# Attention and expert layer on one core: TensorE weighs the older group directly behind the new group's scores and turns the slot's probabilities afterwards

## The chip, the cores and the metric

The kernel runs on one core of one Trainium2 chip. Its time is the device time of one execution in microseconds (us). It is float32 throughout. TensorE is called PE, VectorE DVE, ScalarE ACT, GpSimd POOL and SyncE SP.

## The reference

One decoder layer over x of 16 sequences x 256 positions x 512 features: a self-attention with three softmaxes, a cross-attention with a relative band, and a layer of product-key experts. The change touches the cross-attention alone. Cut to that:

```python
q = (wq @ query + bq); k = (wk @ key + bk); v = (wv @ value + bv)   # 8 heads of 32 channels, 512 positions
scores = einsum('bhqd,bhkd->bhqk', q, k) * scale
scores = scores + skew(einsum('bhqd,rd->bhqr', q, rel_k)) * ...      # a band of 9 offsets
weights = softmax(where(mask == 0, -inf, scores))
context = einsum('bhqk,bhkd->bhqd', weights, v) + band(weights) @ rel_v
out = wo @ context + bo
```

## The kernel before

Everything up to about 1413 us is the attention pass; the expert pass follows it. The attention pass is a software pipeline of rounds over the 16 sequences (b runs from -1 to 17). A round has 32 steps s. In each step every engine takes its part from a list written out by hand (`round_` of each engine, with the table `At` of steps at which the other work stands). Each engine works strictly in its written order; semaphores join them.

A round of the cross-attention makes 32 softmax tiles of 128 queries x 512 keys (8 heads x 4 query tiles), in 8 groups of 4 heads. The path of a tile is:

- **score** (PE, L705): at every fourth step, the four heads of a group at once, each in a 32-row part of the array, into four PSUM banks (h_bank and s_bank in the trace). It waits until DVE has taken the last scores of the group before out of the banks (semaphore `s_emptied`).
- **top_score** (DVE, L1243): adds mask and band and takes the maximum (nmx), one head per step. It waits for the score, and for the exponential of two steps before, whose buffer it writes.
- **exponentials** (ACT, L1054): one per step.
- **turn** (PE, L715): three steps later, four transposes of 128x128 into one of two PSUM banks `t_bank`. The two banks are given out in turn to turns and other products (REL, CK, CQ, CV, PB), so a job waits until the job two before it has been copied out.
- **turned** (ACT, L1060): copies that bank to SBUF. In ACT's list of a step it is the first thing; the exponential stands behind it, and the copies that the self-attention wants (L975, L1022, L1002, L982 and others) stand behind the exponential.
- **weigh** (PE, L731): eight steps behind the score, 16 products in 32-column parts of the array (32 instructions in the trace, two for each) that weigh the values of a whole older group; it needs the turned probabilities up to step s-2 and `linv_kept` (L1065, a copy made two steps before). DVE takes its result one step later (L1261, `evict`).

Between these stand the products of the self-attention of another sequence, which go through one PSUM bank `a_bank`: XN (two sets of transposes, L743, steps 0 and 1), Q (steps 2 to 5), RAW, V, WT (L788, step 12), ATT (steps 13 and 15), OUT (steps 6 and 8), FOLD. Each waits until ACT or DVE has emptied `a_bank` of the one before.

Below, "slot s" is the stretch from the score of step s to the score of step s+4. In slots 16 and 20 (`SCORE_LATE`) PE turns first and scores afterwards, then weighs; in the other slots it scores, turns, weighs.

Of the kernel before, what the change touches and what calls it, by code (L numbers as in the profile page):

```python
# [36 lines left out]
def wait(eng, what, value):  # L37

    if not (isinstance(value, int) and value <= 0):
        eng.wait_ge(what, value)  # L40
# [64 lines left out]
def part(tile, at, *shape):  # L105

    flat = tile[:].rearrange("p a b -> p (a b)") if len(tile.shape) == 3 else tile[:]
    names = "abcd"[:len(shape)]
    return flat[:, at:at + math.prod(shape)].rearrange(f"p ({' '.join(names)}) -> p {' '.join(names)}",
                                                       **dict(zip(names, shape)))  # L110
# [17 lines left out]
def attention_pass(nc, w, kept_stats, early, x3_dram, rows_in, rows_out, rows_laid, fold_dram):  # L128
# [12 lines left out]
    HPT = P // HC  # L141
# [29 lines left out]
    TURN_LAG, SUM_LAG, SPREAD_LAG, WEIGH_LAG, EVICT_LAG = 3, 5, 6, 8, 9  # L171
    TOP_STEPS = 2 * TOPK // 8
    FOLD_VALUES_AT = 16
    SCORE_LATE = (16, 20)
# [7 lines left out]
    def cross_in_round(b):  # L182
        return not isinstance(b, int) or 1 <= b <= B

    def tail_in_round(b):
        return not isinstance(b, int) or 2 <= b <= B + 1
# [4 lines left out]
    def last_cross_round(b):  # L191
        return b == B

    def turn_at(b, s):

        if s >= TURN_LAG:
            return (b - 1, s - TURN_LAG) if cross_in_round(b) else None
        return (b - 2, s - TURN_LAG + STEPS) if tail_in_round(b) else None

    def group_at(b, s, lag):  # L200

        if (s - lag) % HPT:
            return None
        if s >= lag:
            return (b - 1, (s - lag) // HPT) if cross_in_round(b) else None
        return (b - 2, (s - lag + STEPS) // HPT) if tail_in_round(b) else None
# [31 lines left out]
    def t_job(b, kind, n=0):  # L238

        place = t_jobs(b).index((kind, n))  # L240
        known = b if isinstance(b, int) else 2
        return (jobs_before(t_jobs, known) + place) % 2, jobs_before(t_jobs, b) + place
# [14 lines left out]
    with ExitStack() as ctx:  # L257
# [25 lines left out]
        cv = part(early.in_rows, 12352, 2, QT_N, C)  # L283
# [127 lines left out]
        def prob_tile(slot):  # L411

            return probs[:, slot * PROW + WIN:slot * PROW + WIN + L]
# [266 lines left out]
        def _(pe):  # L680
# [5 lines left out]
            def t_open(b, kind, n=0):  # L686

                bank, before = t_job(b, kind, n)
                wait(pe, t_emptied, before - 1)
                return t_bank[bank]  # L690
# [6 lines left out]
            def score(r, s, p):  # L697

                group = s // HPT
                o, t = divmod(group, QT_N)  # L700
                if s == 0:
                    pe.wait_ge(t_emptied, t_job(r, "CQ", CT - 1)[1] + 1)
                wait(pe, s_emptied, r * STEPS + s)
                for g in range(HPT):
                    ins = nc.tensor.matmul(s_bank[g][:, 0:L], cq[g * HC:(g + 1) * HC, 1 - p, o, t * P:(t + 1) * P],  # L705
                                           ck[g * HC:(g + 1) * HC, 1 - p, o, :], start=True, stop=True,
                                           skip_group_check=True)
                ins.then_inc(s_filled, 1)

            def turn(b, s, r, n):  # L710
                bank = t_open(b, "PT", s)
                pe.wait_ge(exp_done, r * STEPS + n + 1)
                src = prob_tile(n % PSLOTS)
                for k in range(QT_N):
                    ins = nc.tensor.transpose(bank[:, k * P:(k + 1) * P], src[:, k * P:(k + 1) * P], ident[:])  # L715
                ins.then_inc(t_filled, 1)

            def spread(r, n):
                wait(pe, acc_emptied, r * GROUPS + n)
                pe.wait_ge(linv_ready, r * GROUPS + n + 1)  # L720
                nc.tensor.transpose(acc, linv_wide[:].rearrange("p g c -> p (g c)"), ident[:]).then_inc(linv_turned, 1)

            def weigh(b, s, r, n, values):

                o = n // QT_N
                pe.wait_ge(linv_kept, r * GROUPS + n + 1)
                pe.wait_ge(t_emptied, t_job(*((b, "PT", s - 2) if s >= 2 else (b - 1, "PT", s - 2 + STEPS)))[1] + 1)
                for k in range(QT_N):
                    for g in range(HPT):
                        h = o * HPT + g  # L730
                        ins = nc.tensor.matmul(acc[g * HC:(g + 1) * HC, :], values[:, k, h * HC:(h + 1) * HC],  # L731
                                               prob_t[:, n % 2, g, k, :], start=(k == 0), stop=(k == QT_N - 1),
                                               skip_group_check=True)
                ins.then_inc(acc_done, 1)
# [86 lines left out]
            def finish(b, s):  # L821

                r = b - 2
                if s == At.PB:
                    bank = t_open(b, "PB")
                    pe.wait_ge(near_packed, r + 1)
                    for t in range(QT_N):
                        ins = nc.tensor.transpose(bank[0:H * REL, t * P:(t + 1) * P],
                                                  near_c[:, t, :, :].rearrange("p h j -> p (h j)"), ident[:])
                    ins.then_inc(t_filled, 1)  # L830
                if s in At.OUT:
                    o = At.OUT.index(s)
                    if o == 0:
                        pe.wait_ge(t_emptied, t_job(b, "PB")[1] + 1)
                        pe.wait_ge(acc_emptied, (r + 1) * GROUPS)
                    bank = a_open(b, "OUT", o)
                    product(bank[:, 0:L], lambda k: cw_o[:, k, o * P:(o + 1) * P], lambda k: cn_t[:, k, :], CT,
                            more=True)
                    nc.tensor.matmul(bank[:, 0:L], rel_out[:, o * P:(o + 1) * P], near_t[:], start=False,
                                     stop=True).then_inc(a_filled, 1)  # L840

            def begin_expert(b, s):
                if s in At.EARLY_TURN:
                    r = At.EARLY_TURN.index(s)
                    bank = a_open(b, "EARLY_TURN", r)
                    pe.wait_ge(early.xn_loaded[r], 16)
                    for k in range(KD):
                        ins = nc.tensor.transpose(bank[:, k * P:(k + 1) * P], early.xn[:, r, k * P:(k + 1) * P],
                                                  ident[:])
                    ins.then_inc(a_filled, 1)  # L850
                if s in At.EARLY_SIMS:
                    c = At.EARLY_SIMS.index(s)
                    bank = a_open(b, "EARLY_SIMS", c)
                    pe.wait_ge(early.fold_back[c], 16)
                    product(bank[:], lambda k: early.xn_t[:, k, :],
                            lambda k: early.fold[:, k, c * BANK:(c + 1) * BANK], KD).then_inc(a_filled, 1)
# [65 lines left out]

            def round_(b, p):
                for s in range(STEPS):
                    if s % HPT == 0 and s not in SCORE_LATE and cross_in_round(b):
                        score(b - 1, s, p)
                    if turn_at(b, s):
                        turn(b, s, *turn_at(b, s))
                    if s in SCORE_LATE and cross_in_round(b):
                        score(b - 1, s, p)  # L930
                    if group_at(b, s, SPREAD_LAG):
                        spread(*group_at(b, s, SPREAD_LAG))
                    if tail_in_round(b):
                        finish(b, s)
                    if group_at(b, s, WEIGH_LAG):
                        weigh(b, s, *group_at(b, s, WEIGH_LAG), cv[:, 1 - p if s >= WEIGH_LAG else p])
                    if last_cross_round(b):
                        begin_expert(b, s)
                    if b == B + 1:
                        for c in range(early.CHUNKS):  # L940
                            if At.NEXT_SIMS[c] == s:
                                next_sims(c)
                    if isinstance(b, int) and b == -1 and s == FOLD_VALUES_AT:
                        fold_values()
                    if second_in_round(b):
                        attend_second(b, s, p)
                    if first_in_round(b):
                        attend_first(b, s, p)
# [994 lines left out]
```

## Time and profile before

| | |
|---|---|
| device time, three runs | 2553.26, 2556.84, 2561.5 us (median 2556.84) |
| profiled execution, first to last instruction | 2553.4 us |
| attention pass, first to last score | 145.3 to 1403.2 us |
| one round (score of step 0 to the next) | 80.85 us |
| PE busy in the program | 2402.2 us (94%) |
| DVE, ACT, POOL busy | 2042.5, 1121.9, 1079.4 us |
| mean granted TensorE clock | 0.984 |

The page gives no device time of the profiled execution apart from its span; the fastest timed run is within 0.2 us of the span. PE's busy time is modelled for pipelined matmuls, so the distance from the start of one piece of work to the start of the next is the safer measure of what it costs.

### The profile page before, as it was taken

The numbers are of one execution on the slowest core, as the hardware profiler recorded it, in microseconds if no ns is written. First come the engines' busy times: TensorE is split into PE (matmuls) and PEld (weight loads), VectorE is DVE, ScalarE is ACT, GpSimd is POOL, SyncE is SP. The second block draws the span as 40 slices with busy tenths as digits, with TensorE's granted clock in tenths as the row PEclk, the third lists the DMA queues.
The fourth block names the chain that finished last, engine by engine and source line by source line (L and its number), as shares of the span: only waits on it lengthen the run. The fifth ranks groups of instructions, "written<-read, shape, count | busy, mean of one in ns | idle before, by whom it ended". The sixth has DMA issues, their size and how long they took to land. (4 is left out here: it accounts for less than half of the span.)

```text
span 2553.4 us, 40781 instructions
## 1 busy us (share of the span) xinstructions
PE 2402.2 (94%) x12856; PEld 1333.3 (52%) x12856; DVE 2042.5 (80%) x5966; ACT 1121.9 (44%) x2612; POOL 1079.4 (42%) x1564
## 2 busy tenths in 40 slices
PE   7889999999999999999989899999999999999985
PEld 5456666656666566666555344444444444444432
DVE  1467776677767776677665699999999999999997
ACT  2257666667666666667666122222122222212221
POOL 1133333333333333334233445555555555555552
PEclk9999999999999999999999999999999999999998
DMA  3035554455545545455458789999999999999996
GB/s 112 15 108 139 163 151 141 134 148 149 155 125 144 162 143 155 114 145 172 135 148 258 272 337 390 392 382 384 382 382 383 385 389 391 383 383 382 385 371 261
DMA packets 292741, 622.47 MB, mean 244 GB/s; under 512 B 162352, under 2 KB 163376, under 8 KB 292528
## 3 DMA queue, kind: packets, MB, share of 16 engines
q0 software_dynamic: 83968, 438.34, 45.2%
q1 hardware_dynamic: 174768, 80.85, 11.9%
q10 hardware_dynamic: 33792, 100.67, 11.7%
q8 instruction: 105, 1.72, 0.3%
q14 instruction: 108, 0.88, 0.1%
HBM read 577.80 MB, written 142.61 MB: 282 GB/s over the span
## 5 line engine op out<-in xcount | busy, mean ns | idle before, releaser
L1544 POOL DMA_INDIRECT out_rows<-rows_out,rows_now x256 | 272.0, 1063 | 373.1 <-PE out_ps L1611 292.5
L1054 ACT ACTIVATE in_rows<-scores,nmx 128x512 f32<-128x512 f32 x512 | 373.2, 729 | 113.8 <-DVE nmx L1243 111.1
L1565 PE MATMUL l_bank<-fold,xn_tf 128*128 128x512 f32 x960 | 421.6, 592 | 0.0
L1060 ACT COPY in_rows<-t_bank 128x512 f32<-128x512 f32 x512 | 298.7, 584 | 214.7 <-PE t_bank L715 213.7
L1535 POOL DMA_INDIRECT in_rows<-rows_in,rows_now x248 | 303.2, 1223 | 128.9 <-DVE hid L1799 63.8
L622 POOL TENSOR_TENSOR added<-mask_add,band 128x136 f32<-128x136 f32 (+1 forms) x512 | 246.7, 483 | 256.4 <-DVE nmx L1243 255.0
L715 PE MATMUL t_bank<-ident,in_rows 128*128 128x128 f32 x2048 | 319.6, 281 | 10.1 <-ACT in_rows L1027 5.1
L715 PEld LDWEIGHTS t_bank<-ident,in_rows 128*128 128x128 f32 x2048 | 237.4, 143 | 171.6 <-issue 100.8
L683 PE MATMUL a_bank<-fold 128*128 128x256 f32 (+1 forms) x1024 | 303.9, 441 | 15.4 <-ACT fold L975 6.9
L1807 DVE CUSTOM_DVE_ANT_0 out_rows<-out_rows,hid 128x1024 f32<-128x1024 f32 x256 | 307.1, 1221 | 3.5 <-ACT hid L1668 3.5
L1655 ACT COPY sims<-l_bank 128x512 f32<-128x512 f32 x120 | 70.2, 585 | 537.2 <-PE l_bank L1565 516.9
L1565 PEld LDWEIGHTS l_bank<-fold,xn_tf 128*128 128x128 f32 x960 | 182.4, 190 | 229.6 <-issue 229.6
L1243 DVE CUSTOM_DVE_ANT_0 scores<-h_bank,added 128x512 f32<-128x512 f32 x256 | 174.6, 688 | 157.8 <-PE s_bank L705 146.3
L1607 PE MATMUL out_ps<-w_out,hid_t 128*128 128x512 f32 x512 | 229.8, 602 | 10.6 <-ACT hid_t L1690 10.6
L683 PEld LDWEIGHTS a_bank<-fold 128*128 128x128 f32 x1024 | 187.5, 191 | 91.5 <-issue 49.5
L1577 PE MATMUL hid_ps<-w_in,xn_kept 128*128 128x512 f32 x512 | 226.9, 596 | 7.5 <-ACTq L1710 6.0
L1799 DVE SCALAR_TENSOR_TENSOR hid<-in_rows,lin,hid 128x1024 f32<-128x1024 f32 x160 | 204.5, 1278 | 0.5
L621 POOL COPY added<-mask_add 128x128 f32<-128x128 f32 (+2 forms) x224 | 71.6, 319 | 314.5 <-DVE nmx L1243 302.7
L1243 DVE CUSTOM_DVE_ANT_0 scores<-s_bank,added 128x512 f32<-128x512 f32 x256 | 175.5, 686 | 33.0 <-ACT in_rows L1054 11.5
L1771 DVE CUSTOM_DVE_ANT_0 in_rows<-in_rows,xn_ring 128x512 f32<-128x512 f32 x256 | 161.2, 683 | 9.6 <-PEq L257 9.6
L1577 PEld LDWEIGHTS hid_ps<-w_in,xn_kept 128*128 128x128 f32 x512 | 97.8, 191 | 131.9 <-issue 131.9
L705 PE MATMUL h_bank<-in_rows 32*128 32x512 f32 x512 | 146.0, 647 | 17.2 <-DVE nmx L1243 14.7
(210 smaller groups left out, 3829.9 us busy)
## 6 DMA issues: line engine op xcount, KB each, us to landing
rows_in<-in_in_b_dram ACTq DMA_DIRECT2D x16, 2048.0 KB, 8.5
rows_out<-in_out_a_dram ACTq DMA_DIRECT2D x16, 2048.0 KB, 9.0
rows_in<-in_in_a_dram ACTq DMA_DIRECT2D x16, 1024.0 KB, 8.3
rows_out<-in_out_b_dram ACTq DMA_DIRECT2D x16, 1024.0 KB, 5.8
rel_scratch<-rel_pad SPq DMA_DIRECT2D x16, 640.0 KB, 3.2
band<-rel_scratch SPq DMA_DIRECT2D x512, 20.0 KB, 2.5
prob_scratch<-in_rows SPq DMA_DIRECT2D x512, 20.0 KB, 2.3
near<-prob_scratch SPq DMA_DIRECT2D x64, 156.1 KB, 3.1
```

The costliest lines, as they stand in the source:

```text
L622: nc.gpsimd.tensor_tensor(added[:, s % 2, lo:hi], mask[:, lo:hi], band[:, group % 2, g, lo - first:hi - first], ALU.add).then_inc(added_re ...
L683: ins = nc.tensor.matmul(out, lhs(k), rhs(k), start=(k == 0), stop=(k == k_tiles - 1 and not more))
L715: ins = nc.tensor.transpose(bank[:, k * P:(k + 1) * P], src[:, k * P:(k + 1) * P], ident[:])
L1054: nc.scalar.activation(prob_tile(s % PSLOTS), scores[:, s % 2, :], ACT.Exp, bias=nmx[:, s:s + 1], scale=-1.0, accum_out=lsum[:, s:s + 1]). ...
L1060: nc.scalar.copy(prob_t[:, n // HPT % 2, n % HPT, :, :].rearrange("p k q -> p (k q)"), bank[:]).then_inc(t_emptied, 1)
L1243: nc.vector.tensor_tensor_reduce(out=scores[:, s % 2, :], in0=s_bank[s % HPT][:, 0:L], in1=added[:, s % 2, :], scale=-1.0, scalar=-NEG, op ...
L1535: nc.gpsimd.indirect_dma_start(in_rows[:, place_in(h, odd), :], None, rows_in, bass.IndirectOffsetOnAxis(rows_now[:, odd, h:h + 1], 0)).th ...
L1544: nc.gpsimd.indirect_dma_start(out_rows[:, h, :], None, rows_out, bass.IndirectOffsetOnAxis(rows_now[:, odd, h:h + 1], 0)).then_inc(out_lo ...
L1565: ins = nc.tensor.matmul(l_bank[c % 2][:], xn_t[:, k, :], fold[:, k, c * BANK:(c + 1) * BANK], start=(k == 0), stop=(k == KD - 1))
L1577: ins = nc.tensor.matmul(hid_ps[:, n * BANK:(n + 1) * BANK], xn_kept[:, k, :], w_in[:, k, n * BANK:(n + 1) * BANK], start=(k == 0), stop=F ...
L1607: nc.tensor.matmul(out_ps[:], hid_t[:, k, :], w_out[:, k, :], start=(k == 0), stop=False, skip_group_check=True)
L1807: nc.vector.tensor_tensor_reduce(out=out_a[:, h, :], in0=out_a[:, h, :], in1=hid[:], scale=1.0, scalar=0.0, op0=ALU.mult, op1=ALU.add, acc ...
```

## The change

PE's list of a step is put in another order. Where a score is made before the turn (steps 0, 4, 12, 24, 28), the weigh of the older group now comes directly behind the score, and the turn behind the weigh. At step 8 the weigh stays where it was, behind OUT. At steps 16 and 20 turn, score, weigh stay as they were. No instruction is added or taken away, and the lists of the other engines are the same.

```diff
             def round_(b, p):
                 for s in range(STEPS):
-                    if s % HPT == 0 and s not in SCORE_LATE and cross_in_round(b):
+                    if s in SCORE_LATE and turn_at(b, s):
+                        turn(b, s, *turn_at(b, s))
+                    if s % HPT == 0 and cross_in_round(b):
                         score(b - 1, s, p)
-                    if turn_at(b, s):
+                    if s not in At.OUT and group_at(b, s, WEIGH_LAG):
+                        weigh(b, s, *group_at(b, s, WEIGH_LAG), cv[:, 1 - p if s >= WEIGH_LAG else p])
+                    if s not in SCORE_LATE and turn_at(b, s):
                         turn(b, s, *turn_at(b, s))
-                    if s in SCORE_LATE and cross_in_round(b):
-                        score(b - 1, s, p)
                     if group_at(b, s, SPREAD_LAG):
                         spread(*group_at(b, s, SPREAD_LAG))
                     if tail_in_round(b):
                         finish(b, s)
-                    if group_at(b, s, WEIGH_LAG):
+                    if s in At.OUT and group_at(b, s, WEIGH_LAG):
                         weigh(b, s, *group_at(b, s, WEIGH_LAG), cv[:, 1 - p if s >= WEIGH_LAG else p])
```

PE's order around step 12, the difference (L788 is WT; the L715 behind it is the turn of step 13):

```order
 L705 MATMUL h_bank<-in_rows 128x512 x2
 L705 MATMUL s_bank<-in_rows 128x512 x2
-L715 MATMUL t_bank<-ident,in_rows 128x128 x4
-L731 MATMUL acc_bank<-in_rows 32x128 x16
+L731 MATMUL acc_bank<-in_rows 32x128 x16
+L715 MATMUL t_bank<-ident,in_rows 128x128 x4
 L788 MATMUL a_bank<-ident,xn_tf 128x128 x4
 L715 MATMUL t_bank<-ident,in_rows 128x128 x4
```

The turn of step 12 has moved behind the sixteen products of the weigh, and now stands directly ahead of WT.

PE's order around step 0, before (L743 is XN, first and second; L721 the spread; L683 the first Q):

```order
L705 MATMUL h_bank<-in_rows 128x512 x2
L705 MATMUL s_bank<-in_rows 128x512 x2
L715 MATMUL t_bank<-ident,in_rows 128x128 x4
L731 MATMUL acc_bank<-in_rows 32x128 x16
L743 MATMUL a_bank<-ident,fold 128x128 x4
L715 MATMUL t_bank<-ident,in_rows 128x128 x4
L743 MATMUL a_bank<-ident,fold 128x128 x4
L715 MATMUL t_bank<-ident,in_rows 128x128 x4
L721 MATMUL acc_bank<-ident,linv_wide 128x128
L683 MATMUL a_bank<-fold 128x256 x4
```

The same place now:

```order
L705 MATMUL h_bank<-in_rows 128x512 x2
L705 MATMUL s_bank<-in_rows 128x512 x2
L731 MATMUL acc_bank<-in_rows 32x128 x16
L715 MATMUL t_bank<-ident,in_rows 128x128 x4
L743 MATMUL a_bank<-ident,fold 128x128 x4
L715 MATMUL t_bank<-ident,in_rows 128x128 x4
L743 MATMUL a_bank<-ident,fold 128x128 x4
L715 MATMUL t_bank<-ident,in_rows 128x128 x4
L721 MATMUL acc_bank<-ident,linv_wide 128x128
L683 MATMUL a_bank<-fold 128x256 x4
```

Only the weigh and the first turn have changed places; the first XN follows the turn instead of the weigh.

PE's order around step 28, the difference (L683 t_bank is the product CK, which takes the bank of the turn of step 28):

```order
 L705 MATMUL h_bank<-in_rows 128x512 x2
 L705 MATMUL s_bank<-in_rows 128x512 x2
-L715 MATMUL t_bank<-ident,in_rows 128x128 x4
-L731 MATMUL acc_bank<-in_rows 32x128 x16
-L715 MATMUL t_bank<-ident,in_rows 128x128 x4
+L731 MATMUL acc_bank<-in_rows 32x128 x16
+L715 MATMUL t_bank<-ident,in_rows 128x128 x8
 L683 MATMUL t_bank<-c_in,cw_k 128x512 x2
```

The turns of steps 28 and 29 now stand one behind the other (x8), and CK comes directly behind them.

## Rows read from the trace of the kernel before

A timeline row gives the start in us, the duration in us, the engine, line, operation, tiles, sizes and count; in brackets, how long the engine had been idle and what ended it. A row of stretches gives its length, the busy time of PE, PE's weight loads, DVE, ACT and POOL (with instructions), the granted TensorE clock, the DMA share and GB/s.

**Rows 1.** The page: busy time, share of the span, instructions.
```profile
PE 2402.2 (94%) x12856; PEld 1333.3 (52%) x12856; DVE 2042.5 (80%) x5966; ACT 1121.9 (44%) x2612; POOL 1079.4 (42%) x1564
```

**Rows 2.** Stretches: a steady round, its DVE part in slot 24, the last round.
```profile
933.42:942.05 8.63, 8.57 (x73) 5.64 (x72) 7.83 (x27) 4.95 (x12) 3.11 (x6) 1.00 0.53 161
870.73:951.58 80.85, 77.69 (x622) 50.03 (x621) 58.97 (x192) 55.16 (x138) 30.00 (x64) 1.00 0.51 146
...
1344.87:1412.80 67.93, 60.20 (x559) 36.19 (x558) 36.79 (x118) 45.30 (x113) 20.97 (x52) 0.97 0.78 242
```

**Rows 3.** Timeline of PE, slot 0 of a steady round.
```profile
870.73 0.70 PE L705 MATMUL h_bank<-in_rows 32*128 32x512 f32 x2
...
871.80 0.66 PE L715 MATMUL t_bank<-ident,in_rows 128*128 128x128 f32 x4
872.39 1.08 PE L731 MATMUL acc_bank<-in_rows 128*32 128x128 f32 x32
...
874.74 0.66 PE L743 MATMUL a_bank<-ident,fold 128*128 128x128 f32 x4 [0.24 <-ACT fold L975]
...
876.41 1.99 PE L683 MATMUL a_bank<-fold 128*128 128x256 f32 x8 [0.30 <-ACT fold L975]
...
880.50 0.70 PE L705 MATMUL h_bank<-in_rows 32*128 32x512 f32 x2
```

**Rows 4.** Timeline of ACT in the same slot 0.
```profile
872.50 0.58 ACT L1060 COPY in_rows<-t_bank 128x512 f32<-128x512 f32 x1 [0.83 <-PE t_bank L715]
872.98 0.72 ACT L1054 ACTIVATE in_rows<-scores,nmx 128x512 f32<-128x512 f32 x1
...
874.10 0.59 ACT L975 COPY fold<-a_bank 128x512 f32<-128x512 f32 x1 [0.30 <-PE a_bank L743]
...
875.07 0.73 ACT L1054 ACTIVATE in_rows<-scores,nmx 128x512 f32<-128x512 f32 x1
...
875.79 0.57 ACT L975 COPY fold<-a_bank 128x512 f32<-128x512 f32 x1
```

**Rows 5.** Timeline of PE, slot 16 of the same round: score, weigh, turn.
```profile
915.57 0.70 PE L705 MATMUL h_bank<-in_rows 32*128 32x512 f32 x2
...
916.64 1.08 PE L731 MATMUL acc_bank<-in_rows 128*32 128x128 f32 x32
917.65 0.66 PE L715 MATMUL t_bank<-ident,in_rows 128*128 128x128 f32 x4
```

**Rows 6.** Timeline of PE, slot 28 of the same round.
```profile
942.12 0.70 PE L705 MATMUL h_bank<-in_rows 32*128 32x512 f32 x2
...
944.79 0.66 PE L715 MATMUL t_bank<-ident,in_rows 128*128 128x128 f32 x4
945.28 1.88 PE L683 MATMUL t_bank<-c_in,cw_k 128*128 128x512 f32 x4
```

**Rows 7.** Timeline of PE, slot 4 of the same round.
```profile
883.17 1.99 PE L683 MATMUL a_bank<-fold 128*128 128x256 f32 x8
885.00 0.60 PE L715 MATMUL t_bank<-ident,in_rows 128*128 128x128 f32 x4
...
885.87 1.89 PE L683 MATMUL a_bank<-fold 128*128 128x256 f32 x8
887.60 0.60 PE L715 MATMUL t_bank<-ident,in_rows 128*128 128x128 f32 x4
...
889.26 1.96 PE L683 MATMUL a_bank<-cn_t,cw_o 128*128 128x512 f32 x4 [0.94 <-ACT fold L982]
```

**Rows 8.** Timeline of PE, slot 12 of the same round.
```profile
906.17 0.70 PE L705 MATMUL h_bank<-in_rows 32*128 32x512 f32 x2
...
910.17 1.98 PE L683 MATMUL a_bank<-fold,xn_kept 128*128 128x512 f32 x4 [0.24 <-ACT xn_kept L1022]
```

**Rows 9.** Timeline of ACT and DVE, slot 12 of the same round.
```profile
909.53 0.59 ACT L1022 COPY xn_kept<-a_bank 128x512 f32<-128x512 f32 x1 [0.30 <-PE a_bank L788]
...
912.26 0.69 DVE L1225 TENSOR_TENSOR x<-a_bank,xn_ring 128x512 f32<-128x512 f32 x1 [1.97 <-PE a_bank L683]
```

## The prediction, made before the changed kernel ran

> **What bounds the kernel now.** First the page: PE is busy for 94% of the span, DVE for 80%, ACT for 44% [rows 1]. The page's chain of waits ends on DVE in the expert pass, which the change does not touch; all 80 changed places lie in the attention pass ahead of it, so that stage has to be read by itself. The view by stretches does it: in a steady round of 80.85 us PE is busy for 77.69, ACT for 55.16, DVE for 58.97, with the TensorE clock at 1.00, its 2.4 GHz level [rows 2]. PE is the bound there, and 3 us of a round are its waits. The timeline of PE says what they are. In slot 0 the second XN and the first Q start the moment ACT has copied the bank out of the way [rows 3]; in slot 4 the first OUT does [rows 7]; in slot 12 the first ATT does [rows 8]. So PE is the busiest, but at those four places ACT's list sets PE's pace. ACT, idle for a third of the round, still has short stretches in which it is last. The timeline of ACT shows why [rows 4]: it first copies the turn of the step (L1060), then makes the exponential (L1054), and only then the copy for which PE waits (L975). A turn that comes later holds up all three.
>
> The round shown stands for thirteen that come 80.7 to 81.2 us apart: these (b = 2 to 14) carry all five changed slots and all of the self-attention; b = 1 has only slots 12, 24 and 28, and b = 15 to 17 are thinner.
>
> **What PE's own work gains.** Durations are read from start to start. Score to what follows is 1.07 us, be that a turn (871.80 - 870.73) or a weigh (916.64 - 915.57); a weigh is 1.01 (917.65 - 916.64) [rows 3, 5]. A turn behind a score is 0.59 (872.39 - 871.80) [rows 3]; a turn behind a weigh is 0.49 (945.28 - 944.79) [rows 6]. A product of eight matmuls behind a weigh is 1.83 (885.00 - 883.17), behind a turn 1.73 (887.60 - 885.87) [rows 7]. Score, turn, weigh, product was 1.07 + 0.59 + 1.01 + 1.83 = 4.50; score, weigh, turn, product is 1.07 + 1.01 + 0.49 + 1.73 = 4.30. That is 0.20 less for a slot in which nothing waits.
>
> Each of those 0.1 us stands where PE goes from 32-row or 32-column parts to another shape. The Trainium skill, "TensorEngine Tiling (Array Packing)", Key Properties, says that changing the tiling mode "drains the TensorE". The old order changes shape four times in a slot (full to score, score to turn, turn to weigh, weigh to full), the new one three times, so the rule speaks for this change, and the rows agree with about 0.1 us at an end of a change. By this rule alone, with nothing else to wait for, the sum would be a gain; it is the first rival.
>
> **What the change delays.** The weigh moves ahead of the turn, so the turn starts 2.08 us after the score instead of 1.07: 1.01 later. ACT starts its copy 0.70 after the turn's start (872.50 - 871.80), the exponential 0.48 after that (872.98), and the next operation 0.72 after the exponential (875.79 - 875.07) [rows 3, 4].
>
> *Slot 0.* Score at 870.73, turn at 872.81, ACT's copy at 873.51, exponential 873.99, XN copy 874.71, done (0.59) at 875.30. PE follows a copy's end by 0.05 (874.10 + 0.59 = 874.69, PE at 874.74). The second XN starts at 875.35 instead of 874.74: +0.61. Behind it ACT makes turn copy (0.48), exponential (0.49) and then the second XN copy: 875.19, 875.68, 876.40, done (0.57) at 876.97; Q starts at 877.02 instead of 876.41, again +0.61. Nothing waits between Q and the next score (880.50), so slot 0 costs **+0.61**, its 0.14 of saved switching swallowed by the wait.
>
> *Slot 12.* Score 906.17, turn 908.25, copy 908.95, exponential 909.43, WT copy 910.15 instead of 909.53 [rows 9], done 910.74, ATT at 910.79 instead of 910.17 [rows 8]: **+0.62**. DVE had waited 1.97 us for that product (L1225) and shifts with it [rows 9]; the top scores of step 15, the score at 915.57 and the second ATT all hang on it, so nothing is given back.
>
> *Slot 28.* CK goes into the bank of the turn of step 28. That turn starts at 942.12 + 2.08 = 944.20, its copy at 944.90, done (0.58) at 945.48, CK at 945.53. It started at 945.28 without a wait [rows 6]: **+0.25**. Before, a weigh lay between the turn and CK and hid the copy; that cover is gone.
>
> *Slot 4.* Score 880.50, turn 882.58, Q 883.07, the turn of step 5 at 883.07 + 1.73 = 884.80 instead of 885.00. ACT has nothing urgent behind the late copy here. The wait of OUT (0.94) hangs on ACT's list of step 5, which begins with that turn, and moves with it [rows 7]: **-0.20**.
>
> *Slot 24.* PE saves 0.20, but the next score (942.12) waits for DVE: from 933.42 to 942.05 DVE's 27 instructions follow one another, 7.83 us busy in 8.63, the rest the short pauses between them, and the score starts 0.07 behind [rows 2, 6]. I take **0**; the bounds are -0.20 (PE alone) and 0.
>
> Queued behind the waiting XN, Q, ATT and CK on PE are the next turns, the spread and the next score; ACT and DVE wait for those with slack of their own. SP and POOL queues are not moved past. DVE gets the weigh's result 0.59 earlier, but behind it stand top scores that need an exponential 1 us later, or PE. That is worth nothing in slots 0, 12 and 28, bounded by 0 and -0.3 a slot.
>
> **The sum.** A steady round: 0.61 - 0.20 + 0.62 + 0 + 0.25 = +1.28 us; thirteen make 16.6. Round b = 1: 0.62 + 0.25 = +0.9. In b = 15 there is no XN and no CK: slot 12 again +0.62, the others within 0.3; I take +0.7. In b = 16 PE is busy for 60.20 of 67.93 us [rows 2], the waits for other engines are long, and I take 0, bounded by -0.4 and +1.2. Together +18.2. On the profiled span of 2553.4 that makes 2571.6; the profiled run stands 3.4 below the median of the three runs, so on the median of 2556.84 it is **2575**.
>
> The unknown term is how closely ACT's three operations follow the late turn. The pauses between ACT's operations differ by up to 0.15 us from place to place. If slots 0, 12 and 28 each lost 0.15 less, a round would be +0.83 and the total 13 x 0.83 + 1.6 = +12; if each lost 0.15 more, +1.73 and +24. The likeliest case's own range is 2567 to 2582.
>
> **Rivals.**
>
> *The switches decide (faster).* If the late copy found cover, in that ACT reached the XN, WT and CK copies in time, slots 0, 12 and 28 would gain 0.14 to 0.15 each (turn behind turn or XN behind turn saves 0.05 instead of 0.10), slot 4 0.20, slot 24 0: 0.63 a round, 9.5 for fifteen rounds, 2547; with slot 24's 0.20 too, 2544. For it: PE is the bound and the switches are real [rows 1, 3, 6, 7]. Against: the brackets "<-ACT fold L975" and "<-ACT xn_kept L1022" show PE waiting already, so there is no slack for ACT's 1.01. It decides once ACT's copy ends 0.6 us or more ahead of the time worked out above. It is the case that the rule of "TensorEngine Tiling (Array Packing)" in the Trainium skill stands for.
>
> *Both signs cancel (no change).* The waits grow by 0.2 to 0.3 instead of 0.6, because top scores or the weigh's earlier release let ACT catch up: 0.25 x 2 + 0.1 - 0.2 - 0.2 = +0.2 a round, 2560. Against: ACT's copy, exponential and copy are one engine's list, and nothing else in it can shrink.
>
> *The delay spreads (much slower).* Each of the 80 turns pays its 1.01 in full, through late exponentials that hold DVE's top scores two steps on: 80 x 1.01 = 81 us, 2638. For it: the score of slot 24's end waits for DVE already. Against: a late exponential is done about 4 us behind the score, DVE is busy for only 58.97 of 80.85 us [rows 2], and in slot 12 it waits 1.97 for PE anyway [rows 9]. Nor need the clock fall: a wait of 0.94 leaves the round at the 2.4 GHz level [rows 2, 7], and the new waits are about 1.0.
>
> **Chances.** Forecast 0.78, switches 0.08, cancelling 0.09, spreading 0.05. A measurement of this kernel tells no change from one of 0.3% or 7.7 us. Faster: 0.08 from the first rival. Same: 0.09 from the second and 0.01 of the forecast's lower edge. Slower: the rest, 0.82. The range leaves out the spreading case and the gain and takes in the cancelling one: 2560 to 2583.
>
> **What the changed profile would show.** In slot 0 the second XN 4.6 us behind the score instead of 4.0 and its wait for L975 about 1.0 us instead of 0.24; the score-to-score distance of slot 0 at 10.4 instead of 9.77; slot 12 at 10.0 instead of 9.40; slot 28 at 9.7 instead of 9.46, with a new wait for ACT L1060 ahead of CK; slot 4 at 11.7 instead of 11.94; slot 24 unchanged at 9.92 with a longer wait for DVE; turns behind weighs at 0.49; a round of 82.1. The expert pass is the same, 18 us later. I am wrong if ACT's XN and WT copies start less than 0.3 us later, if slot 28 has no wait, or if a slot without a changed order (8, 16, 20) changes length.

## The result: slower by 0.8%, and the profile after

| | before | changed |
|---|---|---|
| median of four runs | 2555.05 us | 2574.77 us |
| range | 2550.15 to 2561.5 | 2573.6 to 2575.72 |
| span of the profiled execution | 2553.4 | 2573.9 |
| thirteen full rounds, score to score | 1052.92 | 1071.29 |

The ratio of the runs on record is 1.0083, with a 95% interval from 1.0071 to 1.0096 (about +21 us, from 18 to 25); the two medians above differ by 19.7 us. The forecast was 2575 with a range of 2560 to 2583. In the changed kernel all lines behind the edit are numbered two higher (L975 is now L977, L1022 is L1024, L1060 is L1062).

The view by stretches shows the thirteen full rounds, of before first and then of the changed kernel. Columns: stretch, its length, busy time of PE, weight loads, DVE, ACT, POOL, then the granted clock.

```profile
222.94:1275.86 1052.92, 1010.14 (x8061) 650.38 (x8060) 761.45 (x2464) 714.40 (x1770) 384.42 (x819) 1.00 0.51 145
```

```profile
222.50:1293.80 1071.30, 1000.02 (x8062) 650.24 (x8061) 763.44 (x2463) 710.84 (x1768) 383.68 (x818) 1.00 0.49 142
```

PE's own work became shorter, by 10.1 us in thirteen rounds (its busy time is modelled, so this is rough), and the rounds became longer, by 18.4: so PE waits about 28.5 us more. The clock is at the 2.4 GHz level in both (granted clock 1.00).

Slot 0 of the changed kernel, the timeline of PE (it answers to [rows 3]):

```profile
881.71 0.70 PE L705 MATMUL h_bank<-in_rows 32*128 32x512 f32 x2
...
882.78 1.08 PE L731 MATMUL acc_bank<-in_rows 128*32 128x128 f32 x32
883.79 0.66 PE L715 MATMUL t_bank<-ident,in_rows 128*128 128x128 f32 x4
884.29 0.60 PE L743 MATMUL a_bank<-ident,fold 128*128 128x128 f32 x4
...
886.31 0.66 PE L743 MATMUL a_bank<-ident,fold 128*128 128x128 f32 x4 [0.99 <-ACT fold L977]
...
887.99 1.99 PE L683 MATMUL a_bank<-fold 128*128 128x256 f32 x8 [0.47 <-ACT fold L977]
...
892.08 0.70 PE L705 MATMUL h_bank<-in_rows 32*128 32x512 f32 x2
```

And ACT in the same slot (it answers to [rows 4]):

```profile
884.49 0.59 ACT L1062 COPY in_rows<-t_bank 128x512 f32<-128x512 f32 x1 [1.98 <-PE t_bank L715]
884.97 0.72 ACT L1056 ACTIVATE in_rows<-scores,nmx 128x512 f32<-128x512 f32 x1
885.59 0.19 ACT L1056 ACTIVATION_READ_ACCUMULATOR in_rows<-scores,nmx 128x1 f32 x1
885.69 0.57 ACT L977 COPY fold<-a_bank 128x512 f32<-128x512 f32 x1
```

ACT stands idle for 1.98 us instead of 0.83 until the turn comes; then copy, exponential and XN copy follow without a pause, and the second XN starts 4.60 us behind the score instead of 4.01. Its wait grew from 0.24 to 0.99.

Slot 12 has the same picture: the score is at 917.56 and ATT at 922.16, 4.60 behind it instead of 4.00 (PE; it answers to [rows 8]):

```profile
920.13 0.60 PE L788 MATMUL a_bank<-ident,xn_tf 128*128 128x128 f32 x4
920.57 0.60 PE L715 MATMUL t_bank<-ident,in_rows 128*128 128x128 f32 x4
922.16 1.98 PE L683 MATMUL a_bank<-fold,xn_kept 128*128 128x512 f32 x4 [0.99 <-ACT xn_kept L1024]
```

Slot 28, PE (it answers to [rows 6]), with the one new place at which PE waits for ACT's copy of a turn:

```profile
954.11 0.70 PE L705 MATMUL h_bank<-in_rows 32*128 32x512 f32 x2 [0.24 <-DVE nmx L1245]
...
956.19 1.09 PE L715 MATMUL t_bank<-ident,in_rows 128*128 128x128 f32 x8
957.61 1.95 PE L683 MATMUL t_bank<-c_in,cw_k 128*128 128x512 f32 x4 [0.33 <-ACT in_rows L1062]
959.40 0.60 PE L715 MATMUL t_bank<-ident,in_rows 128*128 128x128 f32 x4
```

ACT's copy of that turn:

```profile
956.88 0.59 ACT L1062 COPY in_rows<-t_bank 128x512 f32<-128x512 f32 x1 [1.51 <-PE t_bank L715]
```

Slot 4, PE (it answers to [rows 7]): the turn behind the weigh takes 0.49 to the next start, the product behind it 1.73, and the wait for ACT ahead of OUT is as long as before, only earlier.

```profile
894.16 0.66 PE L715 MATMUL t_bank<-ident,in_rows 128*128 128x128 f32 x4
894.65 1.89 PE L683 MATMUL a_bank<-fold 128*128 128x256 f32 x8
896.38 0.60 PE L715 MATMUL t_bank<-ident,in_rows 128*128 128x128 f32 x4
...
900.65 1.96 PE L683 MATMUL a_bank<-cn_t,cw_o 128*128 128x512 f32 x4 [0.95 <-ACT fold L984]
```

### The profile page after: what moved, and what is told of

It is laid out like the page before. It is cut to its first block and busy times, and to the rows that moved or that the text cites. A ratio compares the mean times of both kernels' runs of the same rounds, so it can differ in the third digit from the quotient of the medians.

```text
span 2573.9 us, 40781 instructions
## 1 busy us (share of the span) xinstructions
PE 2388.8 (93%) x12856; PEld 1330.3 (52%) x12856; DVE 2044.9 (79%) x5966; ACT 1117.9 (43%) x2612; POOL 1079.0 (42%) x1564
## 3 DMA queue, kind: packets, MB, share of 16 engines
q8 instruction: 105, 1.72, 0.3%
## 5 line engine op out<-in xcount | busy, mean ns | idle before, releaser
L1062 ACT COPY in_rows<-t_bank 128x512 f32<-128x512 f32 x512 | 299.3, 585 | 276.5 <-PE t_bank L715 275.6
L715 PE MATMUL t_bank<-ident,in_rows 128*128 128x128 f32 x2048 | 313.6, 279 | 11.1 <-ACT in_rows L1029 5.1
L683 PE MATMUL a_bank<-fold 128*128 128x256 f32 (+1 forms) x1024 | 303.3, 440 | 17.3 <-ACT fold L977 8.9
L715 PEld LDWEIGHTS t_bank<-ident,in_rows 128*128 128x128 f32 x2048 | 236.1, 142 | 124.5 <-issue 75.5
L683 PEld LDWEIGHTS a_bank<-fold 128*128 128x128 f32 x1024 | 188.0, 192 | 91.8 <-issue 46.9
```

Of the source, the lines that this page charges most:

```text
L683: ins = nc.tensor.matmul(out, lhs(k), rhs(k), start=(k == 0), stop=(k == k_tiles - 1 and not more))
L1062: nc.scalar.copy(prob_t[:, n // HPT % 2, n % HPT, :, :].rearrange("p k q -> p (k q)"), bank[:]).then_inc(t_emptied, 1)
```

## The experiments

One table carries most verdicts: the length of each slot, in us, as the median over the thirteen full rounds, from the start of one score to the next. Most slots repeat to 0.02 from round to round, so differences of 0.1 are plain here, while the whole time of a run scatters by 5 us or more.

```
kernel          s0    s4     s8    s12    s16   s20   s24   s28   13 rounds
before          9.76  11.94  13.73   9.40  8.47  8.16  9.94  9.46  1052.9
changed        10.37  11.75  13.73  10.00  8.47  8.16  9.94  9.88  1071.3
e_4_24          9.76  11.75  13.73   9.40  8.48  8.15  9.93  9.46  1050.1
e_0_12         10.37  11.94  13.73  10.00  8.47  8.16  9.94  9.46  1068.5
e_28            9.76  11.94  13.73   9.40  8.48  8.15  9.93  9.88  1058.2
e_copy_first    9.67  11.75  13.73   9.30  8.47  8.16  9.93  9.88  1053.1
e_copy_before   9.77  11.94  13.73   9.40  8.47  8.16  9.93  9.46  1052.9
e_mask_before   9.77  11.95  13.73   9.40  8.48  8.15  9.81  9.46  1051.2
e_mask_24       9.77  11.94  13.73   9.40  8.47  8.16  9.61  9.46  1048.6
e_best1         9.66  11.75  13.73   9.30  8.48  8.16  9.61  9.46  1043.5
e_best2         9.76  11.75  14.17   8.81  8.47  8.16 10.05  9.44  1049.6
```

The theory: each slot in which PE next wants a bank that ACT empties with the turn's copy (slot 28) or behind it in its list (slots 0 and 12) loses by the late turn, and each slot with no such wait gains 0.2 us, because PE changes once less between its shapes (32-row parts, 32-column parts, the full array). The rivals: PE's new order costs or gains by itself wherever it stands, or the loss spreads through exponentials and DVE.

### One group of steps at a time

The edit makes the choice a table, with the order of `round_` as in the changed kernel:

```diff
+    WEIGH_FIRST = (4, 24)          # e_0_12: (0, 12); e_28: (28,)
-                    if s not in At.OUT and group_at(b, s, WEIGH_LAG):
+                    if s in WEIGH_FIRST and group_at(b, s, WEIGH_LAG):
...
-                    if s in At.OUT and group_at(b, s, WEIGH_LAG):
+                    if s not in WEIGH_FIRST and group_at(b, s, WEIGH_LAG):
```

**Steps 4 and 24.** 

> The new order of PE at steps 4 and 24 alone; 0, 12 and 28 as before. My theory (ACT's queue makes the loss, PE's own work gains): slot 4 at 11.75 us instead of 11.94, slot 24 unchanged at 9.92 to 9.94 in the thirteen full rounds because DVE sets its end, slots 0, 12 and 28 at 9.77, 9.40 and 9.46 as before; in all 16 x -0.20 and some -0.2 twice for slot 24 of the last full and the first thin round: -3.5 us, faster by 0.14%. The rival (the new order costs PE itself time, wherever it stands): slower than before by a quarter to two fifths of the 20 us, +5 to +8 us.

Measured: ratio 0.9989 (0.9978 to 1.0001), -2.8 us with an interval that just reaches no change. The slots settle it: slot 4 at 11.75, slot 24 unchanged, all others as before. The new order is a gain at step 4, where nothing hangs on the turn, and costs nothing at step 24; the rival that it costs PE time wherever it stands falls.

**Steps 0 and 12.** 

> The new order of PE at steps 0 and 12 alone. My theory: slot 0 at 10.37 us instead of 9.77 and slot 12 at 10.00 instead of 9.40, the others as before; thirteen rounds with both and two with slot 12 alone, 13 x 1.20 + 2 x 0.6 = +16.8 us, about 2572. The rival that the loss is spread evenly over all five places gives two fifths of 20 us, +8 us.

Measured: 1.0047 (1.0032 to 1.0062), +12.0 us. The full rounds grew by 15.6 us, 13 x 1.20. The slots are 10.37 and 10.00, as in the changed kernel; the whole came out below the expected 16.8, which lies just outside the interval (8.2 to 15.8 us). In the profiled execution the missing part is outside the full rounds: round b = 16 is 2.5 us shorter than before, because its slot 4 took 9.00 instead of 12.06. No profile shows whether that holds for the other three runs. The evenly spread loss of 8 us is at the other edge of the interval, and the slots exclude it.

**Step 28.** 

> The new order of PE at step 28 alone. My theory: slot 28 at 9.88 us instead of 9.46, as in the changed kernel, all others as before; 14 x 0.42 = +5.9, and about +0.2 in the first thin round: +6 us. It is the term that I had put at 0.25; if the additional 0.17 came from the slots ahead of it (a shifted DVE or ACT), this run, where they are as before, shows 9.71 and +3.6 us.

Measured: 1.0035 (1.0019 to 1.0051), +8.9 us; in the profile 5.3 of it are in the full rounds. Slot 28 is 9.88 with all slots ahead of it as before. So the additional 0.17 is the slot's own.

### The queue of ACT

`e_copy_first` is the changed kernel with this in ACT's `round_`, and nothing else:

```diff
+    COPY_FIRST = (0, 1, 12)
...
+                    if s in COPY_FIRST:
+                        if second_in_round(b):
+                            attend_second(b, s, p)
+                        if first_in_round(b):
+                            attend_first(b, s, p)
                     if cross_in_round(b):
                         exponentials(b - 1, s)
...
-                    if second_in_round(b):
-                        attend_second(b, s, p)
-                    if first_in_round(b):
-                        attend_first(b, s, p)
+                    if s not in COPY_FIRST:
+                        if second_in_round(b):
+                            attend_second(b, s, p)
+                        if first_in_round(b):
+                            attend_first(b, s, p)
```

> The changed kernel, with one thing moved in ACT's list: at steps 0, 1 and 12 the copy of XN or WT out of a_bank stands behind the copy of the turn but ahead of the exponential. My theory: the first XN copy starts 0.48 behind the turn's copy instead of 1.20, so the second XN comes at 3.9 us from the score instead of 4.6, Q at 5.6 instead of 6.29, slot 0 at 9.65 instead of 10.37; slot 12 at 9.3 instead of 10.00; slots 4, 24, 28 as in the changed kernel. Together 13 x -1.42 and -0.7 twice: about -20 us, back to 2555. If PE's order costs time by itself or through DVE, the slots stay at 10.37 and 10.00 and the time at 2574.

Measured: 0.9989 (0.9979 to 0.9999) of before, so the whole loss is back. In the full rounds it is back to 0.2 us: 1053.1 us against 1052.9, slot 28 still long and the others shorter; what goes beyond that lies outside the full rounds (see "Two combinations"). The timelines of PE and then of ACT in slot 0 of this kernel:

```profile
861.55 0.70 PE L707 MATMUL h_bank<-in_rows 32*128 32x512 f32 x2
...
865.45 0.66 PE L745 MATMUL a_bank<-ident,fold 128*128 128x128 f32 x4 [0.29 <-ACT fold L979]
...
867.13 1.13 PE L685 MATMUL a_bank<-fold 128*128 128x256 f32 x4 [0.20 <-ACT fold L979]
```

```profile
864.32 0.59 ACT L1064 COPY in_rows<-t_bank 128x512 f32<-128x512 f32 x1 [1.98 <-PE t_bank L717]
864.81 0.59 ACT L979 COPY fold<-a_bank 128x512 f32<-128x512 f32 x1
865.28 0.74 ACT L1058 ACTIVATE in_rows<-scores,nmx 128x512 f32<-128x512 f32 x1
```

The turn is as late as in the changed kernel (ACT idles 1.98 us for it), but with the exponential out of the way the second XN starts 3.90 us behind the score and Q 5.58, as expected (3.9 and 5.6). Slots 0 and 12 fall to 9.67 and 9.30. This shows the mechanism: the loss there was not in PE's order and not in the late exponential, which is now later still, but in the 0.72 us of exponential ahead of the copy for which PE waits.

The same edit on the kernel before:

> The kernel before, PE's order untouched, with only ACT's XN and WT copies ahead of the exponential at steps 0, 1 and 12. Is the gain of the combined kernel the copies' alone? At step 0 and 12 the turn is early and ACT would wait for XN or WT before the exponential: the copy starts when PE is done, at 3.4 us from the score, as before, so slot 12 stays at 9.40; at step 1 the second XN copy moves ahead of an exponential, Q starts some 0.1 to 0.2 us sooner and slot 0 is 9.6 to 9.7. Then the copies alone are worth 1 to 2 us of the 19 that the combined kernel gained, and the new order of PE at 0 and 12 another 0.1 us a slot on top. If the copies alone bring slot 0 to 9.67 and slot 12 to 9.30, the new order is worth nothing there.

Measured: 0.9998 (0.9987 to 1.0008), slots 9.77 and 9.40, nothing. I had expected 0.1 to 0.2 in slot 0, and missed this: ACT now waits for XN first (1.02 us) and starts the exponential 3.85 us behind the score instead of 2.25, right behind the XN copy. Between the two XN copies stand again one exponential and one turn copy, so the second XN copy begins no sooner. ACT in slot 0 (score at 863.73):

```profile
867.10 0.58 ACT L979 COPY fold<-a_bank 128x512 f32<-128x512 f32 x1 [1.02 <-PE a_bank L745]
867.58 0.73 ACT L1058 ACTIVATE in_rows<-scores,nmx 128x512 f32<-128x512 f32 x1
...
868.76 0.59 ACT L979 COPY fold<-a_bank 128x512 f32<-128x512 f32 x1
```

The second XN copy is 5.03 us behind the score, 5.06 before. The two edits are worth something only together: with both, slots 0 and 12 are 0.1 below before. That is less than the 0.2 of slot 4, where nothing waits: here PE still waits for ACT's two copies (0.29 and 0.20 us in slot 0), and only the 0.1 by which XN is made sooner comes through.

### Who sets slot 24

```diff
-        CV, REL, LOAD_MASK, MASK = (9, 11), 24, 4, 26
+        CV, REL, LOAD_MASK, MASK = (9, 11), 24, 4, 11
```

> The kernel before, with one DVE operation (the mask, 0.44 us, L1235) moved from step 26 to step 11, where DVE waits for PE. My theory of slot 24 (DVE's list sets its end by 0.1 us, PE is right behind): slot 24 at 9.8 us instead of 9.93, the length that it has in the one round in which DVE has no statistics of the next sequence; everything else as before, the whole about -1.5 us. If PE or another engine set it, 9.93 stays.

> The same moved mask, and the new order of PE at step 24 alone. My theory: with the 0.44 us of DVE gone PE sets the end, and its 0.20 is now earned: slot 24 at 9.6 us instead of 9.93, about 13 x -0.32 = -4 us in all. If the new order is worth nothing at this place, slot 24 is as long as with the moved mask alone, 9.8.

Both were run once with a profile; 2554.03 and 2551.27 us say nothing by themselves. Slot 24 is 9.81 with the mask moved and 9.61 with the new order as well. So before, DVE set the end of slot 24 by 0.12 us, and PE's 0.20 is earned only once DVE is out of the way. The changed kernel holds the same proof: in its last full round, where DVE has no statistics to make, slot 24 is 9.61 against 9.81 in the same round of the kernel before.

### Two combinations

**Copies first, order 28 left alone.** PE's new order at 0, 4, 12 and 24, `COPY_FIRST`, and the moved mask.

> What the rows point to: new order of PE at steps 0, 4, 12 and 24, old order at 28, ACT's XN and WT copies ahead of the exponential at steps 0, 1 and 12, the mask at step 11. By the slots already seen: 9.67, 11.75, 13.73, 9.30, 8.47, 8.16, 9.62, 9.46 = 80.16 us a round against 80.87; 14 x -0.7 = -10 us, 2543. If the slots do not add, for instance because slot 24 needs the late start, between -4 and -8.

Measured: 0.9932 (0.9916 to 0.9947), median 2536.4 us: by the ratio 17 us faster than before, and 38 by the medians than the changed kernel. The slots add as expected, 9.4 us in the full rounds, but the whole is more than the expected 10 us, which lies outside the interval (13.5 to 21.5 us less):

```profile
857.94:938.09 80.15, 76.95 (x622) 50.00 (x621) 59.05 (x191) 54.76 (x138) 29.91 (x64) 1.00 0.51 147
215.88:1259.41 1043.53, 1000.40 (x8061) 650.04 (x8060) 762.90 (x2464) 710.29 (x1770) 384.46 (x819) 1.00 0.51 146
```

PE is as short of work as in the changed kernel (1000.4 against 1000.0 us), and now the round is short as well. The rest of the 17 us lies outside the full rounds, and only part of it has a place: the first slot of the first cross-attention round is 9.3 to 9.8 us in all three kernels with `COPY_FIRST` and 11.4 to 12.8 in the others. The traces show the same queue at work. In this slot there is no turn to copy yet; ACT's exponential waits for DVE's top score, and the XN copy stands behind it. With the copy ahead it does not wait for DVE. ACT's first XN copy and PE's first Q, before (score at 145.28) and then in `e_copy_before` (score at 141.56):

```profile
147.28 0.72 ACT L1054 ACTIVATE in_rows<-scores,nmx 128x512 f32<-128x512 f32 x1 [1.21 <-DVE nmx L1243]
148.00 0.57 ACT L975 COPY fold<-a_bank 128x512 f32<-128x512 f32 x1
150.95 3.03 PE L683 MATMUL a_bank<-fold 128*128 128x256 f32 x8 [1.67 <-ACT fold L975]
```

```profile
143.38 0.58 ACT L979 COPY fold<-a_bank 128x512 f32<-128x512 f32 x1 [1.02 <-PE a_bank L745]
145.56 3.59 PE L685 MATMUL a_bank<-fold 128*128 128x256 f32 x8 [0.88 <-ACT fold L979]
```

Q starts 4.00 us behind the score instead of 5.67. It happens once in the program, so it is worth about 2 us. `e_copy_before` has the same gain, and its time (0.5 us less, interval from 3.3 less to 2.0 more) neither shows nor excludes it. For the remaining 6 us or so of this kernel no cause is shown: the stretch ahead of the first score and rounds b = 15 and 16, which wander from profile to profile, were shorter in this one.

**Turn ahead of the score.**

```diff
-    SCORE_LATE = (16, 20)
+    SCORE_LATE = (0, 12, 16, 20, 28)
+    WEIGH_FIRST = (4, 24)
...
-        CV, REL, LOAD_MASK, MASK = (9, 11), 24, 4, 26
+        CV, REL, LOAD_MASK, MASK = (9, 11), 24, 4, 11
```

> Another way to three changes of shape in a slot without a late turn: at steps 0, 12 and 28 the turn comes ahead of the score, as at 16 and 20 (turn, score, weigh), ACT's list untouched; steps 4 and 24 in the new order, the mask at step 11. If the late turn is what costs, slots 0, 12 and 28 keep the 0.1 to 0.2 us of the saved change and lose nothing: about 80.87 - 0.15 - 0.19 - 0.1 - 0.32 - 0.15 = 80.0 us a round, -12 us, 2541. Against it: the score and DVE's top scores come 0.5 us later in these slots; if DVE is short there, the rounds stay at 80.4 or above, -4 to -6 us.

Measured: 0.9980 (0.9968 to 0.9991), -5.1 us, the median round at 80.62 against 80.87: the pessimistic case. The turn (0.4 to 0.5 us) moves into the slot before, so slots are to be read in pairs. 8 and 12 together are 22.98 against 23.13, the saved change of shape. 24 and 28 are 19.49 against 19.40, although with the moved mask 24 alone had been 0.3 shorter, and slot 0 behind them gained nothing, although a turn has left it. There DVE is the one that keeps the distance from the score. ACT and PE in slot 0 (score at 785.87):

```profile
790.21 0.72 ACT L1057 ACTIVATE in_rows<-scores,nmx 128x512 f32<-128x512 f32 x1 [0.49 <-DVE nmx L1246]
790.93 0.56 ACT L978 COPY fold<-a_bank 128x512 f32<-128x512 f32 x1
791.54 1.99 PE L684 MATMUL a_bank<-fold 128*128 128x256 f32 x8 [0.30 <-ACT fold L978]
```

The exponential of step 1 now waits for DVE's top score, and the second XN copy stands behind it: Q starts 5.67 behind the score, 5.68 before.

## Why the prediction was right, and the one term that was not

- *PE's own gain.* Predicted 0.20 for a slot in which nothing waits; slot 4 measured 0.19 in the five kernels that have the order there, slot 24 0.20 with DVE out of the way. The busy time of PE fell by 10.1 us in the full rounds, 0.78 a round.
- *Slot 0:* predicted +0.61, measured +0.60. *Slot 12:* +0.62, measured +0.60. The chain turn, copy, exponential, copy was read from the spacing of rows of before and held to 0.02 us; `e_copy_first` shows that it is the cause. That the new waits came out as predicted was not luck: both the place and the 0.7 us of the exponential were tested.
- *Slot 24:* predicted 0, measured 0, for the predicted reason.
- *Slot 28:* predicted +0.25, measured +0.42. The place and the waiting product were right; the size was not. I had ended the sum at the start of CK and let it start 0.05 behind the copy, as XN does. It started 0.14 behind (copy done at 956.88 + 0.59 = 957.47, CK at 957.61), and the product then took 1.79 to the next start, where the same product unhindered took 1.72 (947.00 - 945.28 before). That is 0.09 + 0.07 of the missing 0.17. Both numbers could have been read before the change from a nearer row than XN's: OUT in [rows 7], a product of the same size that also waits for ACT, starts 0.15 behind the end of ACT's L982 (888.29 + 0.82 = 889.11, OUT at 889.26) and takes 1.79 to the next start (891.05). These three lines are from the kernel before:

```profile
888.29 0.82 ACT L982 ACTIVATE fold<-a_bank,b_g 128x256 f32<-128x256 f32 x2
...
891.05 1.02 PE L839 MATMUL a_bank<-near_t,rel_out 72*128 72x512 f32 x2
...
947.00 0.60 PE L715 MATMUL t_bank<-ident,in_rows 128*128 128x128 f32 x4
```

- *The sum.* Full rounds: 13 x 1.41 = 18.4, predicted 16.6; slot 28 (13 x 0.17 = 2.2) is more than the difference. First cross round +0.8 (0.9), but its agreement is luck: slots 12 and 28 gave +1.0, where 0.9 was forecast, and slots 0 and 8, which go from 11.4 to 12.8 and from 11.2 to 12.7 without `COPY_FIRST`, happened to give +1.35 and -1.58. Round b = 15: +1.9 (0.7), partly because its slots 4 and 20, whose lengths go from 9.9 to 11.3 and from 8.2 to 10.3 over the kernels run here without a pattern, came out 0.7 and 0.6 long. Everything else: +0.6 in round b = 16, -1.2 ahead of the first score, +0.1 behind the last. Together 20.6 (the spans differ by 20.5), against 18.2. That the median met the forecast to 0.2 us is partly luck: before was 2556.84 when I wrote and is 2555.05 with the fourth run, so the time grew by 19.7 and not by 18.2. (The step by way of the profiled span changed nothing: a run's time is 1.8 to 2.0 us more than its span in all runs on record, and what was taken off there was put back with the 3.4.)
- *The rivals.* "The switches decide" fell at slots 0, 12 and 28, and is right of slot 4. The rule behind it (the Trainium skill, "TensorEngine Tiling (Array Packing)", Key Properties) agrees with slot 4, which is 0.19 shorter with one change of shape less; that it is a drain, no row here shows. The rule bears on what PE pays, not on what PE waits for. "The delay spreads" did not happen: slots 8, 16 and 20 kept their lengths to 0.01.

## What to carry to other kernels

Before work on the busiest engine is put in a cheaper order, list who waits for each piece that is moved back, and follow that engine's written order to the next thing that it hands to the busiest one. Here a turn moved back for 0.15 to 0.2 us of cheaper work made slots 0 and 12 each 0.6 us longer, where the late piece stood first in ACT's list and the wanted copy last. The two lists are one schedule: the order on PE and the order on ACT were each worth nothing or less alone in slots 0 and 12, and 0.1 us a slot together. And when a new wait is priced, take the delay from a row of a product of the same kind that already waits.

## What the runs showed that was not expected

- A product that had to wait for ACT starts later than the copy's end by an amount that depends on the product, and why is open. From the end of ACT's work to PE's start it was 0.14 to 0.15 us for CK and in nearly every round for OUT, and 0.05 to 0.06 for XN, Q, ATT and the turns (rounds between 500 and 1200 us of both kernels). ATT has the size of CK and OUT, so size is not the reason.
- Several pieces also take longer to the next start when they had to wait: CK 1.79 instead of 1.72 in slot 28, the Q product behind a wait in [rows 3] 1.83 to the next turn (878.24), against 1.73 unhindered in [rows 7].

```profile
878.24 0.60 PE L715 MATMUL t_bank<-ident,in_rows 128*128 128x128 f32 x4
```

- Slot 4 of round b = 16, in which DVE waits for a transfer (3.71 us in the kernel before, tile `near`, the band of the probabilities), was 9.0 to 14.6 us long over the eleven kernels profiled here. Much of the scatter between these profiles is in that slot and in the stretch ahead of the first score (139 to 145 us).
